# A one-core decoder layer: the work between self-attention and cross-attention issued in another order

## The reference

```
x = x + attention(layernorm(x))       # 16 heads, one shared key/value head, causal, rotary
x = x + cross(layernorm(x), ctx)      # 8 heads of 16, band of 64 each side; relu(out) * ctx, then w_ct
x = x + ffn(layernorm(x))             # ternary weights, 8-bit activations
# cross: qkv = x^T w_in^T + b_in; scores = q k / 4; softmax over the band; o = attn v; o w_out + b_out
```

## Time and profile before

| | us |
|---|---|
| median of 3 runs | 1113.43 (1112.75 to 1116.46) |
| the profiled execution's own time | 1114.96 |
| its span in the trace | 1113.1 |
| PE busy | 1022.3 (92%) |
| DVE, ACT, POOL busy | 795.1, 683.2, 611.5 |

### The profile page before, as it was taken

The page is one execution under the profiler, slowest core; times in us unless marked ns, Lnnn a source line. Parts: engine busy times, 40 slices in busy tenths (PEclk is TensorE's granted clock), DMA queues, the critical chain, the costliest instruction groups (busy, mean ns, idle before and its releaser), DMA issues.

```text
span 1113.1 us, 25333 instructions
## 1 busy us (share of the span) xinstructions
PE 1022.3 (92%) x9636; PEld 779.6 (70%) x9636; DVE 795.1 (71%) x1447; ACT 683.2 (61%) x1223; POOL 611.5 (55%) x601
## 2 busy tenths in 40 slices
PE   5689999999999999999997779999999998699996
PEld 5577778888888888888885557777777765344443
DVE  6578776566665666677764367878787866699995
ACT  5544655545545445465666547777787756588885
POOL 3664676756657576565776214555545435555552
PEclk9789999999999999999998779999999998899999
DMA  9125452424323243344546557878787742000001
GB/s 342 64 94 209 178 203 102 178 76 152 124 105 142 87 152 111 117 146 158 190 167 177 145 126 184 189 178 189 181 186 176 145 108 57 10 30 29 30 30 38
DMA packets 51145, 147.69 MB, mean 133 GB/s; under 512 B 10448, under 2 KB 24272, under 8 KB 39760
## 3 DMA queue, kind: packets, MB, share of 16 engines
q1 hardware_dynamic: 42432, 87.32, 29.4%
q0 software_dynamic: 8064, 58.72, 14.3%
q10 hardware_dynamic: 528, 0.00, 0.0%
HBM read 120.46 MB, written 25.17 MB: 131 GB/s over the span
## 4 chain that ended last, share of the span: by engine, by line
PE 55%; issue 11%; DVE 11%; POOL 9%; DMA 7%; ACT 5%; SPq 2%; POOLq 0%; DVEq 0%; ACTq 0%
PE Qb L233 4%; PE Qb L235 4%; PE Qb L234 4%; PE Yb L318 4%; DMA x_K<-k_parts 4%; PE Yb L320 4%; PE Yb L319 4%; PE XY L1073 4%; POOL x_hg L1478 3%; PE Sm L1012 3%; PE Se L1020 2%; PE Sm L1020 2%; DVE a_turned L698 2%; PE Se L1012 2%; POOL a_ql L566 2%
## 5 line engine op out<-in xcount | busy, mean ns | idle before, releaser
L1640 DVE TENSOR_REDUCE x_mx<-Sm 128x4 f32<-128x768 f32 x128 | 122.3, 956 | 63.2 <-PE Sm L1020 62.2
L233 PE MATMUL Qb<-a_xTh,WqH 128*128 128x256 f32 x512 | 147.9, 289 | 2.9 <-DVE a_vl L758 2.8
L234 PE MATMUL Qb<-a_xTl,WqH 128*128 128x256 f32 x512 | 146.9, 287 | 0.0
L235 PE MATMUL Qb<-a_xTh,WqL 128*128 128x256 f32 x512 | 146.7, 286 | 0.0
L411 ACT ACTIVATE Lb<-Lb 128x512 f32<-128x512 f32 x64 | 37.2, 582 | 169.3 <-PE Ob L305 169.3
L698 DVE TENSOR_TENSOR a_turned<-Qb,sinS 64x512 f32<-64x512 f32 (+1 forms) x144 | 94.9, 659 | 61.3 <-PE Qb L235 45.0
L566 POOL TENSOR_TENSOR a_ql<-a_rot,a_qh 128x512 fp32r<-128x512 f32 x64 | 84.1, 1319 | 96.9 <-ACT a_qh L419 96.8
L584 POOL TENSOR_TENSOR a_pr<-a_pr_plain,a_ph 128x512 fp32r<-128x512 f32 x64 | 83.7, 1308 | 97.3 <-ACT a_ph L399 97.2
L1243 ACT ACTIVATE x_ex<-Se 128x768 f32<-128x768 f32 x128 | 104.0, 813 | 51.7 <-PE Se L1020 51.7
L318 PE MATMUL Yb<-a_WoH,a_oH 128*128 128x512 f32 x256 | 103.6, 405 | 2.8 <-POOL a_oN L562 2.7
L233 PEld LDWEIGHTS Qb<-a_xTh,WqH 128*128 128x128 f32 x512 | 100.4, 196 | 6.8 <-issue 2.2
(11 more groups left out here) (210 smaller groups left out, 2812.3 us busy)
## 6 DMA issues: line engine op xcount, KB each, us to landing
a_WoH<-wo_parts POOLq DMA_DIRECT2D x28, 1024.0 KB, 5.2
a_WoL<-wo_parts POOLq DMA_DIRECT2D x28, 1024.0 KB, 7.1
x_K<-k_parts SPq DMA_DIRECT2D x32, 256.0 KB, 7.6
q_parts<-x_qp SPq DMA_DIRECT2D x16, 384.0 KB, 3.0
k_parts<-x_kp SPq DMA_DIRECT2D x16, 384.0 KB, 3.6
x_Q<-q_parts SPq DMA_DIRECT2D x16, 384.0 KB, 5.3
a_w_stage<-in_gateT SPq DMA_DIRECT2D x8, 704.0 KB, 4.1
x_w_stage<-in_gateT SPq DMA_DIRECT2D x8, 704.0 KB, 5.7
```

The lines of the kernel that those rows point to most:

```text
L233: pe.matmul(out, w_hi(k), xTh[:, k, :], start=(k == 0), stop=False)
L234: pe.matmul(out, w_hi(k), xTl[:, k, :], start=False, stop=False)
L235: mm = pe.matmul(out, w_lo(k), xTh[:, k, :], start=False, stop=(k == KD - 1))
L1640: dve.tensor_reduce(mx[:, half, at:at + 4].rearrange("p (j a) -> p j a", j=2), Sm[:, :, 0:2 * WIN].rearrange("p j (a c) -> p j a c", a=2), ...
```

## The change

No arithmetic changes. What moves, by engine:

- ACT: the `high` parts of row 2 move from (7, 7), ahead of the exponentials of attention's last step, to (G, 0), behind them. `rows_high` and the `middle` parts of rows 0 and 1 move from the end of their step to its beginning, behind the `high` parts. The three copies that set the rows of ones in K (L1400) go away.
- POOL: sets the rows of ones instead, by `memset` (`ones_rows`): K0 in (G, 1) behind attention's last low part, K1 in `step(0)`, K2 in `step(1)`. `rows_low` is issued ahead of `low` in (7, 5) and (7, 6); `low` of row 2's queries moves behind attention's low parts to (G, 0).
- PE: `maximum_scores(0, 1)` moves from (G, 1) to behind `values` in (G, 0); `maximum_scores(0, 2)` goes between the halves (two heads each) of the last but one `out_projection`; `folds` and `maximum_scores(0, 3)` go ahead of the last `out_projection`, `maxima_turned` and `maximum_scores(0, 4)` between its halves. Slots 5 to 7 stay behind attention.
- DVE: `normalised` of rows 1 and 2 and the two 0.9 us `memset`s move; `rest` of row 2 moves to (G, 0); the maxima follow PE's order, and `head_values` now stands between slots 4 and 5, ahead of the addition of the last output.
- PE's wait for the rows of ones is now per buffer of K.

The diff, its core:

```diff
+                if i == HG // 2 - 1 and between is not None:
+                    between()
...
-                beside(g, s)
+                beside(g, s, "scores")
...
+                beside(g, s, "values")
             og, os = before(g, s, 2)
             if real(og):
-                out_projection(og, os)
+                out_projection(og, os, (lambda: beside(g, s, "half")) if late(g) else None)
...
+            if s == 0:
+                wait(pe, k_ones, min(b + 1, len(K)))
             if (b, s) == (0, 0):
-                wait(pe, k_ones, len(K))
...
-        def beside(g, s):
-            if g == G - 1 and s >= 5:
+        def beside(g, s, where):
+            if g == G - 1 and s >= 5 and where == "scores":
                 project(s - 5, 0).then_inc(q_full, 1)
                 project(s - 5, 1).then_inc(k_full, 1)
-            if (g, s) == (G, 0):
+            if (g, s, where) == (G, 0, "scores"):
                 maximum_scores(0, 0)
-            if (g, s) == (G, 1):
+            if (g, s, where) == (G, 0, "values"):
                 maximum_scores(0, 1)
+            if (g, s, where) == (G, 0, "half"):
+                maximum_scores(0, 2)
+            if (g, s, where) == (G, 1, "scores"):
                 rows_values(0)
-                maximum_scores(0, 2)
+                folds()
+                maximum_scores(0, 3)
+            if (g, s, where) == (G, 1, "half"):
+                wait(pe, constants_ready, 1)
+                maxima_turned(0, 0)
+                maximum_scores(0, 4)
...
         first["tensor"](pe, beside)
-        folds()
-        maximum_scores(0, 3)
-        wait(pe, constants_ready, 1)
-        maxima_turned(0, 0)
-        for s in range(4, SLOTS):
+        for s in range(5, SLOTS):
...
-            if g == G - 1 and s >= 5:
-                b = s - 5
-                if where == "gathered":
-                    high(qp, 0, b, q_full, q_kept, q_high)
-                    high(kp, 1, b, k_full, k_kept, k_high)
-                else:
-                    middle(qp, qr, b, q_rest, q_mid)
-                    if b < 2:
-                        middle(kp, kr, b, k_rest, k_mid)
-                        rows_high(b + 1)
-            if (g, s, where) == (G, 0, "end"):
-                for i in range(len(K)):
-                    act.activation(K[i][ROWS:SHIFTED, :, :].rearrange("p h t -> p (h t)"), t["ones"][ROWS:SHIFTED, 0:1].to_broadcast([3, XH * D]),
-                                   ACT.Copy).then_inc(k_ones, 1)
+            if (g, s) in ((G - 1, 5), (G - 1, 6), (G, 0)) and where == "gathered":
+                b = s - 5 if s else 2
+                high(qp, 0, b, q_full, q_kept, q_high)
+                high(kp, 1, b, k_full, k_kept, k_high)
+                if b < 2:
+                    rows_high(b + 1)
+                middle(qp, qr, b, q_rest, q_mid)
+                if b < 2:
+                    middle(kp, kr, b, k_rest, k_mid)
...
+            if b < 2:
+                wait(pool, x1_low, b + 4)
+                ones_rows(b + 1)
...
+        def ones_rows(i):
+            wait(pool, k_ones, i)
+            pool.memset(K[i][ROWS:SHIFTED, :, :], 1.0).then_inc(k_ones, 1)
...
-            if g == G - 1 and s >= 5:
-                b = s - 5
-                low(qp, qr, b, q_mid, q_low)
-                if b < 2:
-                    low(kp, kr, b, k_mid, k_low)
-                    rows_low(b + 1)
+            if (g, s) in ((G - 1, 5), (G - 1, 6)):
+                rows_low(s - 4)
+                low(qp, qr, s - 5, q_mid, q_low)
+                low(kp, kr, s - 5, k_mid, k_low)
+            if (g, s) == (G, 0):
+                low(qp, qr, 2, q_mid, q_low)
+            if (g, s) == (G, 1):
+                pool.wait_ge(*first["outputs_split"])
+                ones_rows(0)
...
-            if g == G - 1 and s >= 5:
-                b = s - 5
-                if where == "joined":
-                    rest(qp, qr, 0, b, q_high, q_low, q_rest)
-                    rest(kp, kr, 1, b, k_high, k_low, k_rest)
-                elif b < 2:
-                    normalised(b + 1)
-                    dve.memset(Vw[b][:, :, :], 1.0).then_inc(cleared, 1)
-                else:
-                    weights_sized()
-                    dve.memset(mx[:, :, :], 0.0).then_inc(cleared, 1)
+                normalised(1)
             if (g, s, where) == (G, 0, "joined"):
                 wait(dve, cleared, 3)
                 maxima(0, 0)
-            if (g, s, where) == (G, 1, "joined"):
+            if (g, s) in ((G - 1, 5), (G - 1, 6), (G, 0)) and where == "joined":
+                b = s - 5 if s else 2
+                rest(qp, qr, 0, b, q_high, q_low, q_rest)
+                rest(kp, kr, 1, b, k_high, k_low, k_rest)
+            if (g, s, where) == (G - 1, 5, "joined"):
+                normalised(2)
+            if (g, s, where) == (G - 1, 6, "joined"):
+                dve.memset(Vw[0][:, :, :], 1.0).then_inc(cleared, 1)
+            if (g, s, where) == (G - 1, 7, "joined"):
+                dve.memset(Vw[1][:, :, :], 1.0).then_inc(cleared, 1)
+                weights_sized()
+                dve.memset(mx[:, :, :], 0.0).then_inc(cleared, 1)
+            if (g, s, where) == (G, 0, "end"):
                 maxima(0, 1)
                 maxima(0, 2)
-            if (g, s, where) == (G, 1, "end"):
+            if (g, s, where) == (G, 1, "joined"):
+                constants_made()
+                maxima(0, 3)
+                maxima(0, 4)
                 head_values(0, 0)
                 head_values(0, 1)
             if (g, s, where) == (G, 2, "joined"):
-                constants_made()
-                maxima(0, 3)
+                maxima_rest(0, 0)
+                maxima(0, 5)
 
         first["vector"](dve, beside)
-        maxima(0, 4)
-        maxima_rest(0, 0)
-        for s in range(5, SLOTS):
+        for s in range(6, SLOTS):
             maxima(0, s)
         for b in range(0, B - 1):
             step(b)
```

More of the change, by code:

```diff
@@ L305, in values, with out_projection @@
             pe.matmul(Ob[:, :], vl[par][:, cols], ph[:, :], start=False, stop=True).then_inc(ol_full, 1)
-        def out_projection(g, s):
+        def out_projection(g, s, between=None):
             u = s // NG
@@ L338, in step @@
                 values(pg, par if s >= 1 else 1 - par, ps)
+            if late(g):
+                beside(g, s, "values")
             og, os = before(g, s, 2)
             if real(og):
-                out_projection(og, os)
+                out_projection(og, os, (lambda: beside(g, s, "half")) if late(g) else None)
             if real(pg) and second:
@@ L827, in attention @@
             "banks_rotated": (rot_ready, done(G - 1, ROTS, ROTS - 1)), "scores_read": (pr_ready, PR0 + G * STEPS),
-            "values_read": (oN_ready, ON0 + G * STEPS), "outputs_read": (x_new, X0 + G * STEPS)}
+            "values_read": (oN_ready, ON0 + G * STEPS), "outputs_read": (x_new, X0 + G * STEPS), "outputs_split": (oL_ready, G * STEPS)}
 CHUNKS = [(c, min(F, c + 512)) for c in range(0, F, 512)]
```

## The result

The changed kernel takes 1101.2 us (median of 4 runs, 1100.78 to 1103.72) against 1113.56 (4 runs). The ratio is 0.9888, with a 95% interval of 0.9869 to 0.9906: 12.5 us less, 10.5 to 14.6. The profiled execution took 1103.72 us, its span is 1101.7. One run of e4 (1157.66 us) and one of e11 (1646.48 us) were slow, at a lower clock, and are left out of the numbers given for e4 and e11.

The account below looks back on a forecast made before the run. PE was taken to wait on attention's chain, held by row 2's parts not yet needed. Gains accumulated along stations (3.5, 4.8, 9.7, 8.7, 12.0 us), giving 1113.4 - 12.0 = 1101.4 us; range 1099 to 1104, chance 0.50.

Parts of the forecast that it names:

- none of over 2 us before slot 0: Sign that the forecast is right: PE has no wait of over 2 us before slot 0.
- Row 1's parts ahead of the logarithm: ACT, attention's steps 5 and 6: values of step 5 start 3.5 us earlier, of step 6 4.8 us earlier in all.
- Row 2's high parts behind the last exponential: ACT before slot 0: last exponential no longer held, worth 4.9 us; slot 0 at 614.1 instead of 623.81, 9.7 us in all.
- From values of step 7 to row 1's first slot: PE: 13.4 us to attention's last matmul (before 12.4), then 8.0 (before 11.25); first slot 12.0 us earlier in all.
- slots 0 to 4 are through, or nearly ... 8.0 us: Attention's last matmul to row 1's first slot: few slots remain, so 8.0 us at 1.2 GHz, 7.0 at 2.4; before 11.25.
- Rows of ones: ACT copies gone, worth 1 us at most, nothing added; POOL memsets of 4.2 us cost 0, at 10.2 us 9.
- Carried to the end: From step(0) on: row 2's K waits at the same distance, so the 12.0 us carry over to the end.
- (b): Rival before slot 0: transfers become the wait, K of row 0 lands late, 3 to 5 us later; 1104.5 to 1107; chance 0.20.
- (c): Rival on POOL: the memset costs 10.2 us and 9 us are given back, 1110; chance 0.05.
- (d): Rival on POOL: memsets become the bound; from 11 us each the gain is gone, at 13 1119 us; chance 0.03.
- (a): Rival on PE: clock stays up, 1098, at most 2 us more, 1096; sign: windows from 594 over 0.95; chance 0.17.
- What I drew from it for slot 0: By the clock rule alone, 1.2 GHz about slot 0 and in the sparse slots after attention: 2 us less gain, 1103.4.

Follow-up runs that it names:

- e4: Kernel before with only row 1's and 2's first parts (rows_high, middle, rows_low, normalised) issued earlier; 1109.61 us, ratio 0.9968.
- e11: Kernel before plus twenty unread matmuls on PE ahead of slot 0, the wait itself left; 1112.82 us, ratio 0.9989.
- e1: Changed kernel with row 2's high and rest parts back in (7, 7), ahead of attention's last exponential; 1109.21 us, ratio 0.9969.
- e5: Kernel before with only row 2's high, rest and middle moved to (G, 0) and its queries' low behind attention's low parts; 1107.07 us, ratio 0.9938.
- e2: Changed kernel with the maxima's slots back where they were, on PE and DVE; 1101.17 us, ratio 0.9898.
- e3: Changed kernel with the rows of ones set by three ACT copies again, no memsets; 1100.8 us, ratio 0.9896.
- e6: Changed kernel with each POOL memset of the rows of ones done three times; 1110.67 us, ratio 0.9983.
- e8: Changed kernel with row 2 normalised in (7, 4), maxima(0, 1) ahead of step 7's product, head_values behind slots 5 and 6; 1099.58 us, ratio 0.9869.
- e10: Changed kernel with e8's DVE order and e9's unread matmuls together; 1100.15 us, ratio 0.9877.
- e9: Changed kernel plus unread matmuls on PE: eleven ahead of values of step 5, three behind each of slots 5 to 7; 1102.36 us, ratio 0.9898.
- e7: Changed kernel with row 2's normalisation on DVE in (7, 4) instead of (7, 5); 1100.36 us, ratio 0.9889.

## Why the prediction was right, and where it was not

The time held (1101.4 forecast, 1101.2 measured), and the stations did within 2 us: values of step 5 at 599.5 (measured 599.17), of step 6 at 608.9 (607.88), slot 0 at 614.1 (613.17), values of step 7 at 616.0 (615.08), the last matmul at 629.4 (ends at about 628.2), row 1's first slot at 637.4 (635.67). Part of the closeness is luck. Row 1's first slot came 13.7 us earlier in the span where I had 12.0; 0.8 us of this is that the changed trace entered the passage earlier, and the medians moved by 12.4. One of my signs failed and contradicted my own walk: "none of over 2 us before slot 0", where I had a wait of 2.6 us and it was 3.04. And the clock of the kernel before was 0.65 to 0.84 in the earlier trace rows, not 0.60 to 0.84.

- *Row 1's parts ahead of the logarithm*: right, 3.1 us at values of step 5 and 5.1 at step 6, counted from the shift, against 3.5 and 4.8. Alone it is worth 3.6 us in time (e4). The new wait was 3.04 us, not 2.6; as supposed, the clock fell behind it (0.85 in that window).
- *Row 2's high parts behind the last exponential*: the mechanism right, the size too small. I had 4.9 us; undone it costs 8.0 (e1), alone it gains 6.9 (e5). I knew that a part of the 12.4 us behind this wait ran at 1.2 GHz, but put no price on it: PE was busy there without a pause, at a clock of 0.75. Without the wait this stretch takes 9.7, and fillers in the wait do the same (e5, e11).
- *From values of step 7 to row 1's first slot*: the sum right, its parts not. I charged 1 us to the first stretch and credited 3.3 us to the slots' new places in the second. The step "slots 0 to 4 are through, or nearly ... 8.0 us" holds as a length (7.53) but not as a gain of the interleaving. (The items that I listed for it add up to 8.75 one behind the other, and to 7.55 with slot 6's scores beside the statistics, as they ran.) With the slots back where they were the passage is as long (e2). Nearly all that the changed kernel gains there, 21.9 us from values of step 7 to row 1's first maxima instead of 24.9, is the clock of the first stretch, 2.7 us in e5 and e11. So the 2.3 us net that I gave the slots belong to the wait for the transfers, and the sum came out because one error stood for the other. Each slot is on the path either way, inside the product or behind it. PE has no idle time inside the product for a slot to fill (in e2 it is busy 9.65 us of 9.65), and from values of step 7 to row 1's first slot it is idle for as long in either order: 5.5 us here, 5.6 in e2.
- *Rows of ones*: cost 0, right (e3). The memset took 3.51 us, not 4.2, and 3.77 once. The price that I had for one of 10 us, 9, was right in size (9.5 in e6), though K0's share of it was nothing.
- *Carried to the end*: row 2's K waits at the same distance, 1.25 us, as forecast. The 12.9 us at row 2 became 10.7 at the end of this profiled span, counted from the shift, and 12.4 in the medians; since the second profile of the same kernel has 1.8 us less over that stretch, this is how executions differ, and no rule of giving back is shown.
- *Rivals.* (b) did not come: K of row 0 landed at 609.1, 4 us before slot 0, and ACT waited 1.20 and 0.34 us. (c) and (d) needed a slow memset. (a) was half right: behind 0.78 and 1.19 us of waiting at slot 0 the clock stayed up, where I had put 1 us. That was not certain: of the eleven traces in which PE waits under 2 us at slot 0, or has fillers in the wait, nine have full clock there, and e8 and e10 have not, with the same waits. In the three with a wait of over 5 us (before, e1, e4) it was down each time. The sign of (a), windows at over 0.95, came in two of the four up to row 1's first slot.

The Trainium skill, "TensorE: Matmul & The Clock Gate", section "What's actually happening", has the throttled state as the default, which activity releases. What I drew from it for slot 0, 1.2 GHz there too, did not come: the windows from 604.78 to 628.14 show 1.00. Behind attention, where I drew the same, it is 0.67. The traces of e9 and e11 agree with the sentence: work that nobody needs kept the clock at 1.00.

## What to carry to other kernels

A wait of an in-order engine for work that nobody needs yet can cost more than its length, here 2.7 us behind a wait of 5.27: look at the clock of the dense stretch behind it, and charge the slow matmuls to the wait. A short wait can go either way: behind the same one, two traces can have either clock. Moving work into another stretch gains only if the engine is idle there; add the two stretches up before crediting it. To tell 1 us on 1100, compare stations within a trace, counted from the last point that the change does not touch, and take a second profile of the same kernel before believing in what is given back later.

## What was not expected of the hardware

DVE's normalisation of row 2 took 4.61 us in the changed kernel. The same operation took 0.54 us in the kernel before, when POOL was idle:

```profile
596.25 0.54 DVE L1624 TENSOR_SCALAR x_x<-X,scale,shift 128x512 f32<-128x512 f32 x1
```

The changed kernel, DVE, then POOL beside it:

```profile
590.76 4.61 DVE L1638 TENSOR_SCALAR x_x<-X,scale,shift 128x512 f32<-128x512 f32 x1
595.30 0.68 DVE L732 TENSOR_TENSOR a_oN_plain<-Ob,a_rl 128x512 f32<-128x512 f32 x1
```

```profile
590.54 1.04 POOL L597 TENSOR_TENSOR Dg<-ident,a_negm 32x512 fp32r<-32x512 f32 x1
591.55 1.28 POOL L1437 TENSOR_TENSOR x_x1L<-x_x,x_x1H 128x512 fp32r<-128x512 f32 x1
592.80 1.16 POOL L1441 TENSOR_TENSOR x_qp<-x_qr,x_qp 128x512 bf16<-128x512 f32 x1
593.92 1.16 POOL L1441 TENSOR_TENSOR x_kp<-x_kr,x_kp 128x512 bf16<-128x512 f32 x1
```

It started while POOL ran four operations back to back and ended 0.3 us behind the last one; the product of step 4 waited for it. Moved ahead to (7, 4) it went with two others of its kind in 3.39 us for the three (e7):

```profile
586.34 3.39 DVE L1638 TENSOR_SCALAR x_x<-X,scale,shift 128x512 f32<-128x512 f32 x3
```

There POOL was busy with other low parts too, and 1.1 us each is above the 0.54, but the stall of 4.61 us is gone and values of step 5 start 0.4 us earlier. The Trainium skill, "GPSIMD Engine Reference", section "Key points", names a cause that would fit: POOL shares its interfaces to SBUF with VectorE, with contention where a VectorE instruction runs in a two-port mode or has two inputs in SBUF. The trace agrees in that the operation lasted as long as POOL's row did; whether it ran in such a mode, no run here shows. DVE's addition to x and its maxima of attention's scores, which have an operand in PSUM, took 0.64 and 0.70 us beside busy POOL in the same trace (587.51 and 586.88), as long as elsewhere in the span (medians 0.65 and 0.72).
